# A transformer stack with a one-expert mixture: phases 1 and 2 in one block, rows gathered by a slot table

## What is computed

```python
x = x + gated_linear_attention(layernorm(x))       # 16 heads of 8, chunks, sigmoid gate, RMS norm, Wo
x = x + moe(layernorm(x))
x = x + conv_scan(layernorm(x))                    # in-projection, 4-tap convolution, decay scan, out-projection
x = x + fp4_ffn(layernorm(x))                      # blockwise FP4 of x, weights and hidden
# moe, for each of 4096 tokens a:
e    = argmax(a @ router)                          # 8 experts, one taken
g    = sigmoid(max(a @ router))
moe  = (silu(g*a @ w1[e]) * (g*a @ w3[e])) @ w2[e] # width 352
     + (silu(a @ ws1) * (a @ ws3)) @ ws2           # shared expert, width 352
```

## Time and profile before

| | |
|---|---|
| median of 3 runs | 652.1 us (651.47 to 652.75) |
| profiled execution | 653.99 us, its span 652.3 us |
| TensorE matmul busy | 551.6 us (85%) |
| VectorE, ScalarE, GpSimd busy | 438.3, 307.8, 355.2 us |
| granted TensorE clock, mean | 0.936 |

### The profile page before, as it was taken

One profiled execution on the slowest core, in us unless ns is written; L12 is line 12 of the kernel. 1 busy time (PEld: TensorE's weight loads), 2 busy tenths in 40 slices (PEclk: granted clock), 3 DMA queues, 4 the chain that ended last, 5 costly groups with the idle time before them and its releaser, 6 DMA issues. The chain is left out here.

```text
span 652.3 us, 15280 instructions
## 1 busy us (share of the span) xinstructions
PE 551.6 (85%) x4468; PEld 445.9 (68%) x4469; DVE 438.3 (67%) x1172; ACT 307.8 (47%) x862; POOL 355.2 (54%) x550
## 2 busy tenths in 40 slices
PE   2799999999999379991799999278899999999965
PEld 1457676776776258871689999266778778778754
DVE  2678999999885155552284343126899899899883
ACT  1356666666574224430245444124545645655632
POOL 4468877878776248885400000445667767764221
PEclk9999999999999659996699999778899999999987
DMA  7000000000004551111422111110011011010000
GB/s 200 16 20 33 19 26 25 16 32 16 23 26 108 158 196 34 32 34 43 116 58 57 56 56 40 33 16 10 10 32 18 16 32 17 16 25 15 10 17 16
DMA packets 41686, 28.12 MB, mean 43 GB/s; under 512 B 5232, under 2 KB 38192, under 8 KB 41648
## 3 DMA queue, kind: packets, MB, share of 16 engines
q1 hardware_dynamic: 36016, 23.46, 12.2%
q0 software_dynamic: 5632, 4.20, 3.7%
HBM read 14.01 MB, written 9.44 MB: 36 GB/s over the span
## 5 line engine op out<-in xcount | busy, mean ns | idle before, releaser
L821 PE MATMUL a_ps_a<-a_qx,a_kt 32*128 32x512 f32 x512 | 70.8, 643 | 1.2 <-DMA a_qx<-a_qs 1.0
L1493 POOL DMA_INDIRECT x<-yg_dram,pos x32 | 58.1, 1815 | 11.9 <-issue 11.9
L895 POOL TENSOR_TENSOR d_hq<-d_fh_v,d_fh_scale 128x352 f32<-128x352 f32 x32 | 27.9, 889 | 57.6 <-DVE d_fh_v L921 57.6
L361 POOL TENSOR_SCALAR_AFFINE_SELECT a_at<-a_at 128x512 f32<-128x512 f32 x80 | 50.5, 650 | 11.8 <-ACT a_at L423 11.5
L1317 DVE TENSOR_TENSOR c_hid<-c_act,c_ps 128x352 f32<-128x352 f32 x40 | 20.7, 520 | 44.4 <-ACT c_act L1274 35.7
L423 ACT ACTIVATE a_at<-a_ps_a 128x512 f32<-128x512 f32 x80 | 44.5, 600 | 11.7 <-PE a_ps_a L821 10.1
L1498 POOL MEMSET d_hs<- 128x256 f32 x1 | 0.3, 311 | 88.3 <-POOLq L1177 88.3
L821 PEld LDWEIGHTS a_ps_a<-a_qx,a_kt 32*128 32x128 f32 x512 | 32.1, 192 | 17.9 <-issue 17.2
L1274 ACT ACTIVATE c_act<-c_ps 128x352 f32<-128x352 f32 x40 | 18.5, 463 | 49.6 <-PE c_ps L190 49.2
L1002 POOL DMA_INDIRECT xg_dram<-xn,pos x32 | 35.3, 1104 | 11.9 <-DVE pos L1091 6.2
L188 PE MATMUL d_ps_A<-d_xnT,wmix 128*128 128x256 f32 x128 | 38.4, 300 | 1.6 <-DVE d_xnT L1672 0.9
(11 more groups left out here) (274 smaller groups left out, 1807.3 us busy)
## 6 DMA issues: line engine op xcount, KB each, us to landing
a_qx<-a_qs SPq DMA_DIRECT2D x64, 64.0 KB, 1.9
b_w<-in_L_ffn_w_eDF_dram SPq DMA_DIRECT2D x2, 1408.0 KB, 8.1
xg_dram<-a_zero SPq DMA_DIRECT2D x40, 64.0 KB, 1.6
c_rows<-xg_dram SPq DMA_DIRECT2D x20, 128.0 KB, 2.1
yg_dram<-c_y SPq DMA_DIRECT2D x20, 128.0 KB, 1.8
out_dram<-x SPq DMA_DIRECT2D x16, 128.0 KB, 1.9
w<-in_L_ffn_w_eFD_dram SPq DMA_DIRECT2D x2, 512.0 KB, 5.1
x<-in_L_attn_x_dram SPq DMA_DIRECT2D x1, 768.0 KB, 5.7
```

Source lines behind the costliest of these rows:

```text
L361: nc.gpsimd.affine_select(at[:, t, r, :, :], at[:, t, r, :, :], pattern=[[0, 4], [1, P]], compare_op=ALU.is_ge, fill=0.0, base=0, channel_ ...
L821: last = nc.tensor.matmul(ps_a[:, r, :, :], kt[rows, b.par, c_, tile(t)], qx[rows, b.par, :, c_, tile(t)], start=(c_ == 0), stop=(c_ == 1))
L895: return eng.tensor_tensor(self.by(to), self.by(self.v[:, :]), self.spread(self.scale), ALU.mult)
L1493: nc.gpsimd.indirect_dma_start(out=x[:, t, :], out_offset=None, in_=g["yg_dram"][:, :], in_offset=bass.IndirectOffsetOnAxis(ap=g["pos"][:, ...
```

## The change

Phases 1 and 2 become one block, `phase_ab`. The single buffer `xn2s` is now stored to `xn2_dram` by SyncE, and `normed` waits until the store of the batch before has landed; the copy `xn2`, the zero stores and the scatter are gone. Groups 0 and 1 of the shared expert are placed among the steps of the last batch, the routing follows from group 2 on. `slot_table`: for each slot position the token's number and gate, formed by TensorE as products of one-hot matrices (`slot_low` by GpSimd, `slot_high` by VectorE). The expert weights come through a ring of five buffers. In phase 3 GpSimd gathers the rows of each pair by the slot's tokens from `xn2_dram`, and VectorE multiplies them by the gate ahead of the transposes. The diff, its core:

```diff
+            xn2_rows = g["xn2_dram"].rearrange("(t p) d -> p t d", p=P)
+
+            def store(b):
+                if not live(b):
+                    return
+                done(sp, s_xn2, b)
+                sp.dma_start(xn2_rows[:, f_tiles(b), :], xn2s[:, :, :]).then_inc(s_xn2s, 16)
+
             def body(j):
-                done(sp, s_qs, j)
-                apart(sp)
-                done(sp, s_a, j, n=8, per=8, ago=2)
...
+                if live(j):
+                    done(sp, s_qs, j)
+                    apart(sp)
+                    done(sp, s_a, j, n=8, per=8, ago=2)
+                    if j.off == 0:
+                        sp.wait_ge(s_zero, 2)
+                    for h in range(4):
+                        sp.dma_start(qx[h::4, j.par, h, :, :].rearrange("p c n -> p (c n)"),
+                                     qs[h::4, j.par, :, :].rearrange("p c n -> p (c n)")).then_inc(s_qx[j.par], 16)
+                store(j + -3)
...
+            store(Seq(B - 3))
+            sp.wait_ge(s_val, 2 * B)
+            for expert in range(WRING):
+                for n, w in enumerate(("L0_ffn_w1_eDF", "L0_ffn_w3_eDF")):
+                    sp.dma_start(w13[:, expert, n, :], io[w][expert, :, :]).then_inc(s_w13, 16)
+            store(Seq(B - 2))
+            store(Seq(B - 1))
             for f, (f0, fn) in enumerate(FT):
                 sp.dma_start(g["w2"][0:fn, :, f, :],
                              io["L0_ffn_w2_eFD"][:, f0:f0 + fn, :].rearrange("e f d -> f e d")).then_inc(g["s_w"], 16)
-            sp.wait_ge(s_zero, 3)
-            for s in range(SLOTS):
-                sp.dma_start(g["xg_dram"][P * s:P * (s + 1), :], zero[:, :]).then_inc(g["s_w"], 16)
-            sp.wait_ge(g["s_w"], 16 * (4 + 3 + SLOTS))
+            for expert in range(WRING, EXPERTS):
+                sp.wait_ge(s_wl, expert - WRING + 1)
+                for n, w in enumerate(("L0_ffn_w1_eDF", "L0_ffn_w3_eDF")):
+                    sp.dma_start(w13[:, expert - WRING, n, :], io[w][expert, :, :]).then_inc(s_w13, 16)
+            sp.wait_ge(g["s_w"], 16 * (4 + 3))
+            sp.wait_ge(s_xn2s, 16 * B)
...
-                copy_xn2(j + -2)
...
+            pool.wait_ge(s_pos, 2)
+            for part in range(4):
+                for t in range(8 * part, 8 * part + 8):
+                    last = nc.gpsimd.tensor_scalar(slot_low[:, t, :], small[:, SLOTS + EXPERTS:SLOTS + EXPERTS + P],
+                                                   low_pos[:, t:t + 1], None, ALU.is_equal)
+                last.then_inc(s_part, 1)
...
+                if s_stored is not None:
+                    done(act, s_stored, b, n=16, per=16, ago=1)
...
+                normed(j + -1, xn2s, rstd2, shift2, s_nb2, (s_xn2p,), s_xn2, s_xn2s)
...
+            copied(Seq(B - 1), 1, 3)
+            copied(Seq(B - 1), 1, 1)
+            token_high(1)
+            normed(Seq(B - 2), xn2s, rstd2, shift2, s_nb2, (s_xn2p,), s_xn2, s_xn2s)
+            transposed2(Seq(B - 2))
+            gated_up(0, 0)
+            squares(Seq(B - 1))
+            gated_up(0, 1)
+            gated_up(0, 2)
+            gated_up(1, 0)
+            scored(Seq(B - 2))
+            normed(Seq(B - 1), xn2s, rstd2, shift2, s_nb2, (s_xn2p,), s_xn2, s_xn2s)
+            gated_up(1, 1)
+            transposed2(Seq(B - 1))
+            token_high(2)
+            gated_up(1, 2)
+            scored(Seq(B - 1))
+            for n in range(2, GROUPS):
+                for f in range(3):
+                    gated_up(n, f)
+                    if f == 0 and n + 1 < GROUPS:
+                        token_high(n + 1)
+                if n == 2:
+                    act.wait_ge(s_hot, 1)
+                    nc.scalar.activation(gate, best, ACT.Tanh, scale=0.5).then_inc(s_gate, 1)
+                expert_high(n - 2)
+            for expert in range(GROUPS - 2, EXPERTS):
+                expert_high(expert)
...
+            def positions():
+                dve.wait_ge(s_r, 1)
+                step(nc.vector.tensor_scalar(over, ps_n, float(P - 1), None, ALU.add))
+                step(nc.vector.tensor_scalar(count, over, 7, 7, ALU.arith_shift_right, ALU.logical_shift_left))
+                step(nc.vector.tensor_tensor_scan(upto, ones[:, 0:EXPERTS], count, 0.0, ALU.mult, ALU.add))
+                step(nc.vector.tensor_tensor(base, upto, count, ALU.subtract))
+                step(nc.vector.tensor_tensor(rank, ps_r, base.unsqueeze(2).to_broadcast(spread), ALU.add))
+                step(nc.vector.tensor_tensor(rank, rank, hot, ALU.mult))
+                step(nc.vector.tensor_reduce(posf, rank.rearrange("p e t -> p t e"), AX.X, ALU.add))
+                nc.vector.tensor_copy(g["pos"][:, :], posf)
+                step(nc.vector.tensor_copy(posi, posf))
+                step(nc.vector.tensor_scalar(hii, posi, 7, 7, ALU.arith_shift_right, ALU.logical_shift_left))
+                nc.vector.tensor_copy(hif, hii).then_inc(s_pos, 1)
+                nc.vector.tensor_tensor(low_pos, posf, hii, ALU.subtract).then_inc(s_pos, 1)
+
+            def slot_columns():
+                by_slot = [P, T, SLOTS]
+                dve.wait_ge(s_pos, 2)
+                step(nc.vector.tensor_tensor(slot_high[:, :, SLOTS:], hif.unsqueeze(2).to_broadcast(by_slot),
+                                             small[:, 0:SLOTS].unsqueeze(1).to_broadcast(by_slot), ALU.is_equal))
+                step(nc.vector.tensor_tensor(slot_high[:, :, 0:SLOTS], slot_high[:, :, SLOTS:],
+                                             small[:, SLOTS + EXPERTS + P:].unsqueeze(2).to_broadcast(by_slot), ALU.mult))
+                dve.wait_ge(s_gate, 1)
+                step(nc.vector.tensor_scalar(gate, gate, 0.5, 0.5, ALU.mult, ALU.add))
+                nc.vector.tensor_tensor(slot_high[:, :, SLOTS:], slot_high[:, :, SLOTS:],
+                                        gate.unsqueeze(2).to_broadcast(by_slot), ALU.mult).then_inc(s_pos, 1)
...
+            masked(Seq(B - 1), 1, 2)
+            token_low(1)
+            hidden(0, 0)
+            gated(Seq(B - 1))
+            hidden(0, 1)
+            mean_square(Seq(B - 1))
+            residual(Seq(B - 1))
+            done(dve, s_x2, Seq(B - 1))
+            norm_stats(Seq(B - 1), stats2, s_st2)
+            norm_aggr(Seq(B - 1), stats2, mv2, s_st2, s_nb2, s_ln2)
+            hidden(0, 2)
+            hidden(1, 0)
+            hidden(1, 1)
+            add(0)
+            token_low(2)
+            hidden(1, 2)
+            one_hot()
+            for n in range(2, GROUPS):
+                for f in range(3):
+                    hidden(n, f)
+                    if f == 0 and n + 1 < GROUPS:
+                        token_low(n + 1)
+                    if (n, f) == (2, 2):
+                        positions()
+                        slot_columns()
+                    if (n, f) == (4, 1):
+                        slot_experts()
+                    if (n, f) == (5, 2):
+                        slot_table()
+                add(n - 1)
+                expert_low(n - 2)
+            add(GROUPS - 1)
+            for expert in range(GROUPS - 2, EXPERTS):
+                expert_low(expert)
...
+            def slots(part):
+                if part == 0:
+                    pe.wait_ge(s_pos, 3)
+                pe.wait_ge(s_part, part + 1)
+                for t in range(8 * part, 8 * part + 8):
+                    last = nc.tensor.matmul(ps_s, slot_low[:, t, :], slot_high[:, t, :], start=(t == 0), stop=(t == T - 1))
+                if part == 3:
+                    last.then_inc(s_tab, 1)
...
+            run_skewed(pe, body, -2, 4, 14, B - 2)
+
+            scores(Seq(B - 3))
+            values(Seq(B - 1), 0)
+            state(Seq(B - 1))
+            transposes2(Seq(B - 2))
+            up(0, 0)
+            values(Seq(B - 1), 1)
+            up(0, 1)
+            finish(Seq(B - 1))
+            up(0, 2)
+            up(1, 0)
+            scores(Seq(B - 2))
+            down(0, 0)
+            up(1, 1)
+            down(0, 1)
+            transposes2(Seq(B - 1))
+            up(1, 2)
+            scores(Seq(B - 1))
+            group(2)
+            count_and_rank()
+            group(3)
+            group(4)
+            slots(0)
+            slots(1)
+            group(5)
+            slots(2)
+            slots(3)
+            group(6)
+            group(7)
+            down(7, 0)
+            down(7, 1)
...
-            def load(j):
-                done(sp, s_xp, j, ago=2)
-                sp.dma_start(rows[:, j.par, :, :], dram_rows(g["xg_dram"], j)).then_inc(s_rows[j.par], 16)
...
+            def gather(k):
+
+                done(pool, s_xp, Seq(k), ago=2)
+                for t in range(2):
+                    nc.gpsimd.indirect_dma_start(
+                        out=rows[:, k % 2, t, :], out_offset=None, in_=g["xn2_dram"][:, :],
+                        in_offset=bass.IndirectOffsetOnAxis(ap=g["slot_token"][:, 2 * k + t:2 * k + t + 1], axis=0),
```

(67 more changed lines are left out.)

370 lines of the change are left out of this document (128 added, 242 removed).

## The result

The changed kernel takes **720.8 us** (717.8 to 723.3, four runs) against 652.4 us for the kernel before (651.5 to 653.9, four runs beside it): a ratio of 1.104, with a 95% interval of 1.100 to 1.109. Forecast were 714 us, within 676 to 745. The profiled execution took 721.1 us, with a span of 719.3.

What follows compares the result with a forecast made beforehand. TensorE was taken to bound the loops of phases 1 and 3, where only waits reaching it cost time. Terms +32.5 + 6 - 12 + 35.8 = +62.3 on the profiled execution gave 716.3, less 1.9 to the median: 714 us, range 676 to 745.

Steps and rivals of the forecast that it cites:

- The ring of the store: Phase 1 batch loop: normed waits for a store queued behind copies that wait for queries; period 14.15 against 11.65, +32.5 us.
- Q to N: Batch loop: end of queries(b+2) on GpSimd to start of normed(b) on ScalarE; 4.45 us instead of 1.74.
- N to Q: Batch loop: start of normed(b) on ScalarE to end of queries(b+3) on GpSimd; taken as 9.7 us.
- N(1): Start of normed into xn2s for batch 1 on ScalarE, phase 1; placed at 60.19 + 4.45 us, before at 61.93.
- The clock in the loop: Phase 1: TensorE idles some 2.5 us per batch and its granted clock falls; +6 us, bounds nothing and 22.
- my quarter: Phase 1: share taken of the upper bound of 22 us, a clock loss of 1.7 us in each of 13 batches; +6.
- The seam: Between phases 1 and 2: the new order starts the shared expert's group 2 at 229.3 instead of 249.60; -20.3 us.
- N(13): Start of normed into xn2s for batch 13 on ScalarE, phase 1; forecast at 234.4 us against 201.95.
- Phase 2's additions: Phase 2, on top of its six groups: count_and_rank 1.3, slots 7.4, VectorE's slot columns block 7.2 with clock; +15.9 us.
- End of block: Behind phase 2's last down: phase 3 starts after 3 us instead of 10.7, as the scatters go.
- Phase 3: Transposes wait for the gate product, pairs 6.3 us instead of 4.60, and a later start; +35.8 us, bounds 28 and 43.
- Phase 4: Last phase: untouched by the change, only shifts in time; no gain or loss.

Runs made afterwards that it cites:

- experiment 4: Kernel before, plus only SyncE's store of xn2s behind the copies and normed's wait for the previous batch's store: 696.4 us, 1.066 of the kernel before.
- A: Changed kernel with VectorE's gate product in phase 3 moved ahead of the two hid: 696.0 us.
- experiment 1: Changed kernel with SyncE issuing the store of xn2s ahead of the four copies instead of behind them: 673.5 us, 1.031 of the kernel before.
- experiment 2: Changed kernel with the store of xn2s put between the second and third of the four copies: 695.0 us.
- experiment 3: Changed kernel with ten extra constant transposes per batch on TensorE, ahead of transposes2 where it waits for ScalarE: 716.3 us.
- experiment 6: Changed kernel with store ahead of copies, gate product ahead of hid, slot_columns cut in three, and earlier buffer clearing and gathers on GpSimd: 638.2 us, 0.980 of kernel before.
- B: Changed kernel with both the store ahead of the copies and the gate product ahead of hid: 648.9 us, 0.996 of the kernel before.

## Why the prediction was right

**The ring of the store** (+32.5): right in mechanism, and in the sum partly by luck. Q to N was taken as 4.45 us and is 4.72: the copies hold SyncE 2.65 us, not 2.45, and the landing is 1.94, not 1.8. N to Q was taken as 9.7 and is 9.74 at full clock. A batch at full clock is 14.4 to 14.5 us, forecast 14.15; over the twelve batches that is about +33 against 11.67 of before, where the forecast had +30. The missing 3 us are made up at the start: the forecast put N(1) at 60.19 + 4.45 = 64.6, 2.7 us later than before, and it came at 61.21, 0.7 earlier. In experiment 4 N(1) is at 64.81, as forecast; that the changed kernel's profile started early is nothing that the prediction had, and so luck.

**The clock in the loop** (+6) is the term that was too small. The fall came in seven of twelve batches and cost 1.7 us or more each time; 15.52 less 14.45 is 1.07 us a batch, 13 us, double my quarter. The price of one fall was right, how often it comes was a guess between bounds of 0 and 22. Of twelve batches, six ran partly at the low clock in A, whose loop is the same.

**The seam** (-20.3): -18.3. In experiment 1, with the clock at 1.00 in the first 15 us of the seam, group 2 starts 26.7 us after N(13) (229.09 - 202.38), that is -20.9 against the kernel before; in the changed kernel the clock averages 0.77 there and group 2 starts after 29.4. The 2.7 us between them I put down to the low clock, a term that I had priced for the loop only: 0.23 of 15 us is 3.5. Experiments 2 and 3 lie between, with a granted clock of 0.86 and 0.85 from N(13) to N(14) and 28.3 and 28.4 us from N(13) to group 2. The last store landed in time under its cover, as placed: from 269 us to the start of group 2 the timeline shows no wait of TensorE but the last 0.37 us.

**Phase 2's additions** (+15.9): +13.4. `count_and_rank` 1.1 (283.73 to 284.85; forecast 1.3), `slots` twice 3.49 = 7.0 (7.4), VectorE's block 4.71 and some 1.2 of a fallen clock (5.5 and 1.7). One statement was wrong without effect: the Tanh of the gate brought no table load; the only one of phase 2 is the first Silu's.

**End of block**: phase 3 starts 3.46 us after the last `down`, forecast 3.1. The saving is -7.2, forecast -7.6.

**Phase 3** (+35.8): +36.4. From its start, transposes(3) at +24.2 (forecast 23.9), transposes(4) at +32.3 (31.7), a pair 6.32 (6.3), transposes(19) at +127.2 (126.6). First transposes came at +5.95, not +4.2. A gather issues in 0.98 us in the mean, not 1.3, but the first took 1.24 and the next followed 0.30 later, so the rows were there at +4.12, not +3.7. Then the two gate products took 1.77 us (345.20 to 346.97), not 0.42: one of them lasted 1.57 us, while GpSimd issued a gather and cleared a buffer. In experiment 6, where the buffers are cleared before, both took 0.48 us together. What held it was not tested. This cost nothing, as transposes(3) waits for gather(3), which stands behind the weights anyway.

**Phase 4** was forecast to shift only and took 2.8 us less. Over the nine programs it varies by 3.8 us with the same code. The granted clock goes with it in part: 0.94 and 0.93 in the two shortest, 0.90 in the three longest, but also 0.93 at 236.7 us in A. In the comparison it is luck, and in my favour: up to the start of phase 4 the changed kernel is 69.8 us late, 7.5 more than the sum.

The sum: forecast +62.3, measured +67.0 between the profiled spans. The difference of 4.7 is made up of +7.0 from the loop, +2.0 from the seam, -2.5 from phase 2, +1.0 from the two stretches behind it and -2.8 from phase 4.

**The two rules that were weighed.** By the Trainium skill (DMA: Bandwidth & Descriptors, Anatomy of one DMA) the store would have cost an estimated 2.3 us and the term 6.5 us more. That section is headed as the path of DMAs issued from GpSimd, and its fit was measured there; the store is issued by SyncE, so the estimate was stretched. The trace has 1.94 us from issue to N, and experiment 2 has 1.95, so the row was nearer; the latency was paid once a batch. By the Trainium skill (ScalarE: Activation LUTs, What ACT_TABLE_LOAD costs) a drain of 1.38 us goes with the load; in the rows of phase 2 above the load follows the last copy at once (261.94 + 0.38 = 262.32, load at 262.33), takes 1.28 us, and Silu starts 0.02 us later. No drain shows here, and the row decides.

## What to carry to other kernels

An in-order engine that issues transfers is part of every ring that a transfer's completion closes: before adding a wait for one, write down what stands ahead of it on its queue and what that in turn waits for. Here one moved line gives back 47 us of 68 and a second 25, with the same data, buffers and waits; the regrouping was sound, and with both lines and two smaller moves it is about 2% faster than the kernel before. Where a change gains at a seam and waits in a loop, price the loop first: the 25.5 us gained at the two seams, of which phase 2's additions took back 13.4, were outweighed by 3.85 us in each of twelve batches, 46 us.

## What was not expected of the hardware

DMAs of 64 and of 128 KB took about the same time from issue to landing (the page's part on DMA issues of the changed kernel: KB each, median us):

```profile
a_qx<-a_qs SPq DMA_DIRECT2D x64, 64.0 KB, 1.9
xn_dram<-a_xn2s SPq DMA_DIRECT2D x16, 128.0 KB, 1.8
```

The clock fell less often than the idle stretches came: in the changed kernel TensorE stood still for 2.3 to 3.1 us in every batch, and seven of twelve ran partly at the low clock. Where the stretch was 1.2 to 1.7 us (experiment 3), none of the last eight did; in experiment 2 one batch, behind 1.81 us, ran at 0.88, and the ten after it, behind 1.0 to 1.6 us, at 1.00. What decides whether a given stretch is followed by a fall stays open. Also left open: in the changed kernel N(0) came 3.5 us earlier than before (46.96 against 50.48), in experiment 1 it did not (50.33). The same code varies there from one profile to the next: A, whose phase 1 is that of the changed kernel, has N(0) at 48.69 and N(1) at 62.99 (61.21 in the changed kernel), and B, whose phase 1 is that of experiment 1, has 48.35 and 60.50 (62.49 in experiment 1).
